# Spreading the softmax denominators of three head groups through DRAM in a one-core decoder kernel

## The reference

```python
att = jnp.einsum('bhqd,bhkd->bhqk', q, k) * scale
att = jnp.where(causal[None, None], att, -jnp.inf)
y = jnp.einsum('bhqk,bhkd->bhqd', jax.nn.softmax(att, axis=-1), v)
attc = jnp.einsum('bhqd,bhkd->bhqk', qc, kc) * scale
y = y + jnp.einsum('bhqk,bhkd->bhqd', jax.nn.softmax(attc, axis=-1), vc)
y = y.transpose(0, 2, 1, 3).reshape(x.shape[0], T, C)
return y @ Wp + bp
```

## Time and profile before

| what | value |
|---|---|
| median of 3 runs | 2014.0 us (2013.98 to 2019.18) |
| profiled execution, its own time | 2022.06 us |
| its span, first to last instruction | 2020.2 us |
| TensorE busy | 1575.8 us (78%) |
| VectorE busy | 1434.7 us (71%) |
| ScalarE busy | 833.2 us (41%) |
| GpSimd busy | 654.7 us (32%) |
| mean granted TensorE clock | 0.889 |

### The profile page before, as it was taken

One profiled execution on the slowest core, in us unless ns is written; L12 is line 12 of the kernel. 1 busy time (PEld: TensorE's weight loads), 2 busy tenths in 40 slices (PEclk: granted clock), 3 DMA queues, 4 the chain that ended last, 5 costly groups with the idle time before them and its releaser, 6 DMA issues. The chain is left out here.

```text
span 2020.2 us, 19779 instructions
## 1 busy us (share of the span) xinstructions
PE 1575.8 (78%) x6792; PEld 757.8 (38%) x6792; DVE 1434.7 (71%) x2096; ACT 833.2 (41%) x1570; POOL 654.7 (32%) x423
## 2 busy tenths in 40 slices
PE   4796799884987699874977799855567898669985
PEld 2353332232544222242544223232232222348874
DVE  6996778657995878468986877389968776333324
ACT  4541246645442166644432365543312566322211
POOL 2664501212763401125653211227635021112221
PEclk9898789996998699987998699988987899769998
DMA  5910722003001820002004520021007220127753
GB/s 167 342 51 0 177 41 41 1 1 116 17 1 49 168 34 8 2 32 98 4 0 123 94 40 2 1 84 43 0 0 159 38 41 1 64 89 252 232 180 127
DMA packets 121189, 147.46 MB, mean 73 GB/s; under 512 B 15429, under 2 KB 103886, under 8 KB 119040
## 3 DMA queue, kind: packets, MB, share of 16 engines
q1 hardware_dynamic: 117344, 137.53, 25.4%
q0 software_dynamic: 3744, 8.66, 1.2%
HBM read 96.79 MB, written 50.79 MB: 73 GB/s over the span
## 5 line engine op out<-in xcount | busy, mean ns | idle before, releaser
L168 PE MATMUL PS<-arena 128*32 128x512 f32 (+11 forms) x4150 | 884.4, 453 | 105.2 <-DVE maxs L1724 24.4
L168 PEld LDWEIGHTS PS<-arena 128*32 128x32 f32 (+3 forms) x4150 | 368.9, 128 | 597.7 <-ACT arena L1705 276.4
L1705 ACT ACTIVATE arena<-PS 128x512 f32<-128x512 f32 (+3 forms) x768 | 375.4, 541 | 379.9 <-PE PS L168 378.7
L1354 POOL TENSOR_TENSOR arena<-arena 128x1024 f32<-128x1024 f32 x128 | 305.0, 2384 | 238.0 <-DVE arena L1380 140.4
L1724 DVE TENSOR_REDUCE maxs<-PS 128x1 f32<-128x1024 f32 x256 | 302.1, 1216 | 80.9 <-PE PS L168 80.8
L1380 DVE TENSOR_TENSOR_SCAN arena<-PS,arena 128x1024 f32<-128x1024 f32 x128 | 292.2, 2283 | 6.1 <-ACT PS L1329 6.1
L168 PE MATMUL PS<-arena,ident 128*128 128x512 f32 (+1 forms) x560 | 260.1, 590 | 5.4 <-DVE arena L1389 5.4
L1329 ACT ACTIVATE PS<-arena,A_neg 128x511 f32<-128x511 f32 x256 | 165.9, 681 | 237.4 <-DVE arena L1380 188.0
L1558 POOL TENSOR_TENSOR arena<-xn 128x512 f32<-128x512 f32 x16 | 20.2, 1266 | 590.9 <-ACT xn L1693 590.9
L1389 DVE TENSOR_TENSOR arena<-arena,PS 128x1024 f32<-128x1024 f32 x128 | 156.3, 1221 | 7.3 <-PE PS L168 3.2
L168 PE MATMUL PS<-bc,bc_sel 96*128 96x512 bf16 x128 | 52.5, 410 | 120.0 <-DVE arena L1389 113.5
(11 more groups left out here) (261 smaller groups left out, 1796.6 us busy)
## 6 DMA issues: line engine op xcount, KB each, us to landing
arena<-in_ew SPq DMA_DIRECT2D x46, 512.0 KB, 4.9
arena<-stack_parts SPq DMA_DIRECT2D x288, 64.0 KB, 3.9
rows_in<-nil SPq DMA_DIRECT2D x16, 1088.0 KB, 12.5
arena<-b_rows SPq DMA_DIRECT2D x16, 1024.0 KB, 7.6
stack_parts<-arena SPq DMA_DIRECT2D x40, 384.0 KB, 3.1
arena<-stack_parts SPq DMA_DIRECT2D x96, 128.0 KB, 4.7
arena<-rows_in SPq DMA_DIRECT2D x23, 272.0 KB, 5.4
arena<-picked_rows SPq DMA_DIRECT2D x16, 256.0 KB, 3.2
```

The source lines that it names most:

```text
L168: return nc.tensor.matmul(o, l, r, start=start, stop=stop)
L1354: nc.gpsimd.tensor_tensor(b_sb[i % 2], u[:, 2 * kh:2 * kh + 2, :], Brow[:, n, :].unsqueeze(1).to_broadcast([P, 2, T]), ALU.mult).then_inc( ...
L1705: nc.scalar.activation(probs[(HG * s + h) % NPR][:, 0:N], bank(4 + n % 2)[:, 0:N], ACT.Exp, scale=HD ** -0.5).then_inc(S["ring_read"], 1)
```

## The change

TensorE and ScalarE no longer spread the denominators of groups 0 to 2. When ScalarE has copied a group's sums, SyncE stores the four denominator rows of `Y1` and `Y2` to a DRAM tensor `dens`, waits for both stores, and loads each of its two halves into `den_sb` with every row repeated 32 times. GpSimd waits for the loads (`dens_in`). The last group keeps the selector matmuls and copies; its copy also waits for the inverse of group 2. The ring's numbering loses the tiles of the removed matmuls, by twos, so the banks still alternate as before. The semaphore `bp_added`, for which nothing waited, is gone.

```diff
+    dens = nc.dram_tensor("dens", (2, HG, T), F32).ap()
...
         def ring(g, k, h):
-            return HG * (STEPS * g + k) + h + 2 * max(g - 1, 0) + (2 if g >= 1 and k >= 2 else 0)
+            return HG * (STEPS * g + k) + h
 
-        def ring_den(g, i):
-            return HG * STEPS * (g + 1) + 2 * g + i + (2 * HG if g + 1 < NG else 0)
+        def ring_den(i):
+            return HG * STEPS * NG + i
...
+                def load_denominators(g):
+                    sp.wait_ge(S["pv_copied"], g + 1)
+                    for i, y in enumerate((Y1, Y2)):
+                        sp.dma_start(dens[i], y[HD:P:32, :]).then_inc(S["dens_out"], 16)
+                    sp.wait_ge(S["dens_out"], 32 * (g + 1))
+                    for i in range(2):
+                        sp.dma_start(den_sb[:, i, :], dens[i].unsqueeze(1).to_broadcast([HG, 32, T]))\
+                            .then_inc(S["dens_in"], 16)
+
                 sp.wait_ge(S["pv_mm"], STEPS)
+                load_denominators(0)
                 load_stacks(sp, 3)
-                load_max_rows(2)
+                load_max_rows(2, (0,))
+                load_max_rows(2, (1,))
+                load_denominators(1)
                 load_max_rows(3)
+                load_denominators(2)
...
                 for g in range(NG):
-                    pool.wait_ge(S["ring_read"], ring_den(g, 1) + 1)
+                    if g + 1 < NG:
+                        pool.wait_ge(S["dens_in"], 32 * (g + 1))
+                    else:
+                        pool.wait_ge(S["ring_read"], ring_den(1) + 1)
...
-                        if k == 1 and g >= 1:
-                            denominators(g - 1)
                         if k >= 1:
                             values(g, k - 1)
...
                 values(NG - 1, STEPS - 1)
-                denominators(NG - 1)
+                last_denominators()
...
-                def copy_denominators(g):
+                def copy_last_denominators():
+                    act.wait_ge(S["norm_ready"], NG - 1)
...
-                    if g >= 1 and k == 1:
-                        copy_denominators(g - 1)
                 copy_sums(NG - 1)
-                copy_denominators(NG - 1)
+                copy_last_denominators()
```

More of the change, by code:

```diff
@@ L298, in decoder @@
             bc3_ready dt_mm abs_done sp_ready cn_mm gen_in pow_mm pow_ev b_src_ready b_stored b_ready a_done
-            h_done g_done y_mm y_read u_ready outproj_mm bp_added qkv_mm hi_f_ready mid_ready parts_ready v_mm
+            h_done g_done y_mm y_read u_ready outproj_mm dens_out dens_in qkv_mm hi_f_ready mid_ready parts_ready v_mm
             v_init v_ready ones_ready max_mm max_done mt_mm mt_read mparts_ready ring_mm ring_read pv_mm
@@ L915, in tensor @@
                     if ends:
-                        pe.wait_ge(S["ring_read"], ring_den(NG - 1, 1) + 1)
+                        pe.wait_ge(S["ring_read"], ring_den(1) + 1)
                     for m in range(2 * DT):
@@ L1474, in gpsimd @@
                 pool.wait_ge(S["xn_ready"], TT)
-                nc.gpsimd.tensor_tensor(x1[:], x1[:], bp[:].unsqueeze(1).to_broadcast([P, TT, DM]), ALU.add)\
-                    .then_inc(S["bp_added"], 1)
+                nc.gpsimd.tensor_tensor(x1[:], x1[:], bp[:].unsqueeze(1).to_broadcast([P, TT, DM]), ALU.add)
                 for i in range(len(TILES)):
@@ L1612, in scores, with last_denominators @@
                         last.then_inc(S["ring_mm"], 1)
-                def denominators(g):
-                    pe.wait_ge(S["pv_copied"], g + 1)
+                def last_denominators():
+                    pe.wait_ge(S["pv_copied"], NG)
                     for i, y in enumerate((Y1, Y2)):
-                        pe.wait_ge(S["ring_read"], ring_den(g, i) - 1)
-                        mm(bank(4 + ring_den(g, i) % 2), den_sel[:], y, True, True).then_inc(S["ring_mm"], 1)
+                        pe.wait_ge(S["ring_read"], ring_den(i) - 1)
+                        mm(bank(4 + ring_den(i) % 2), den_sel[:], y, True, True).then_inc(S["ring_mm"], 1)
                 def values(g, k):
@@ L1687, in copy_sums @@
                     nc.scalar.activation(Y2, bank(7), ACT.Copy).then_inc(S["pv_copied"], 1)
-                def copy_denominators(g):
+                def copy_last_denominators():
+                    act.wait_ge(S["norm_ready"], NG - 1)
                     for i in range(2):
-                        n = ring_den(g, i)
+                        n = ring_den(i)
                         act.wait_ge(S["ring_mm"], n + 1)
```

## The result

| | before | with the change |
|---|---|---|
| median | 2015.26 us (4 runs, 2013.98 to 2019.18) | 2036.72 us (4 runs, 2034.54 to 2040.1) |
| ratio | | 1.0101, 95% interval 1.0082 to 1.012 |
| profiled execution, its span | 2022.06, 2020.2 us | 2034.54, 2032.8 us |
| TensorE busy | 1575.8 us | 1551.1 us |

A forecast was written before the change was run, and what follows sets the result against it. TensorE was taken to set the pace in the attention. Against a median of 2014.0 us, minus 15.3, plus 13.6, minus 8.4, plus 9.8 made -0.3, so 2013.7 us, range 1989 to 2027.

The forecast's parts named there:

- Minus 15.3, plus 13.6: Groups 1 and 2: 15.3 us won by removing the selector matmuls, 13.6 given back to late denominators.
- 8 x 1.7 = 13.6: VectorE's reciprocal in groups 1 and 2: denominators 1.7 us late in each of eight places, 13.6 us lost.
- The rest costs nothing: the 24 stack loads ... start some 3.5 us later: Stack loads behind the denominator loads: their later start costs nothing, since their group begins more than 30 us after them.
- four engines, and the way to them: Denominator loads: a source with outer count 4 uses 4 DMA engines, so both land in 7.1 us.
- Rival 1: Denominator loads run on 16 engines, nothing is given back and no clock falls: 1990.3 us, chance 0.18.
- what the removal gives in groups 1 and 2: Heads of groups 1 and 2: removing the selector matmuls wins 1.91 us on TensorE in each of eight places.
- I expect the fall to stay and to cover values and scores in their place: Head of group 3: slow clock remains after the matmuls go, gain 2.1 us in each of four places, 8.4 in all.
- the bound of 3.5 each: Head of group 3: upper bound of the gain in each of four places, if the clock fall disappears.
- the falls behind the new pauses: Groups 1 and 2, after TensorE's wait: clock falls cost 1.6 us each, six of eight places, 9.8 us.
- Rival 3: Groups 1 and 2: denominators 3.2 us late, the pause exceeds what was removed, slower at 2028.7 us, chance 0.22.

The follow-up runs named there:

- e11: The kernel of e1 with the denominator loads cut into four of 128 KB, each with 2 source rows outermost: 2059.34 us, ratio 1.021.
- e2: The changed kernel with each group's denominators loaded by four transfers, one per head, instead of two: 1983.43 us, ratio 0.9862.
- e1: The changed kernel with SyncE waiting for both denominator loads to land before issuing group 3's stack loads: 2011.1 us, ratio 0.9991.
- e3: The changed kernel without the stores and loads of the denominators, so not the full computation: 1984.51 us, ratio 0.9861.
- e10: The kernel of e2 with the selector matmuls and copies returned for group 2 alone: 2001.16 us, ratio 0.9932.
- e4: The changed kernel with VectorE's reciprocal behind the next group's first twelve maxima instead of eight: 1998.15 us, ratio 0.9921.
- e6: The changed kernel with the edits of e1 and e4 together, loads still on four engines: 1988.38 us, ratio 0.9863.
- e8: The changed kernel with the context keys' loads issued last among group 3's stack loads: 2036.15 us, ratio 1.0105.

## Why the prediction was wrong

**The step that failed: "Minus 15.3, plus 13.6".** The term "8 x 1.7 = 13.6" took one lateness for groups 1 and 2. It was 2.0 us in group 2 (1.8 to 2.0 in the four batches) and 8.2 in group 1 (7.9 to 8.6): 4 x 2.0 + 4 x 8.2 = 41 us instead of 13.6. The price of a microsecond of lateness was right (in e11, 7.5 us late, a group takes 49.9 - 40.1 = 9.8 us more, of which 7.5 are the wait and the rest is taken for the slow clock behind it). The error stood in "The rest costs nothing: the 24 stack loads ... start some 3.5 us later": I asked what the new transfers do to the stack loads and not what the stack loads, issued right behind, do to the new ones, and priced a transfer by b_rows, which nothing disturbs. The trace of before had the warning. Its busy time by stretch in group 1, while only the stack loads move:
```profile
311.50:321.50 10.00, 9.40 (x49) 2.33 (x48) 6.80 (x5) 6.68 (x13) 4.98 (x4) 1.00 1.02 150
```
DMA share 1.02 at 150 GB/s: these 24 loads keep all 16 engines busy for some ten microseconds, at a rate well below the 1024 KB in 2.5 us of the earlier trace rows. A load issued just ahead of them was bound to run among them, and that had no term in the sum.

**Right: four engines, and the way to them.** From the 4 short packets of the earlier trace rows I took 4 against 16, and worked out 7.1 us to the landing and a lateness of 1.7; measured, with no stack load near, were 7.3 to 7.7 to GpSimd's start, a lateness of 2.0, and 25.4% of 16 engines. The Trainium skill's rule (DMA: Bandwidth & Descriptors, "Why a DMA increments its semaphore by 16 and not by 1"), that the slowest dimensions of both sides set the number, agrees with the times of e2, e1 and e11. For 4 engines the busy share shows it; for e11 it does too (12.9% of 16 in 362.5 to 372.5, 2.1 engines). For e2 the time alone speaks. Rival 1, 1990.3 with 16 engines, is the kernel e2: 1983.4, and the difference is mostly group 3's.

**Right: what the removal gives in groups 1 and 2.** 41.93 - 40.10 = 1.83 us a group in e3, against 1.91.

**Mis-sized: group 3.** "I expect the fall to stay and to cover values and scores in their place", 2.1 us each. In the change the fall went with the matmuls: 39.1 - 35.1 = 4.0 us (3.8 without the chance part above), about 16 us in all instead of 8.4, even beyond the bound of 3.5 each. e10 brings fall and loss back. Where a fall did come without them (e4, e6), it cost 1.1 to 1.3 us, near the 3.5 - 2.1 = 1.4 that the forecast had for one over values and scores; what it had wrong is that the fall would come each time. The pause before is nearly the same in both kernels; compare the two stretches of the change from group 3's pause on with the earlier trace rows, third and fourth row:
```profile
395.60:399.00 3.40, 2.18 (x14) 0.64 (x13) 2.45 (x4) 3.40 (x7) 0.00 (x0) 1.00 0.00 0
399.00:402.40 3.40, 2.67 (x14) 0.56 (x13) 0.00 (x0) 2.62 (x6) 0.00 (x0) 1.00 0.03 8
```
Nor did the pause alone bring the fall: in the eight places with the matmuls the clock fell between 0.4 us before and 0.9 us after the first of them began. Nor does TensorE's busy time in the pause decide it: it was 2.21 of 3.40 us in e2, without a fall, and 2.21 of 3.40 before the fall in e6. With the selector matmuls TensorE also stands idle some 0.3 us more just before them (1.92 busy in e10), and that was not tried by itself. Why it falls in the one and seldom in the other wasn't settled.

**Right: the falls behind the new pauses.** The stretches of the change around the pause of group 2 (first two) and of group 1:
```profile
368.30:371.70 3.40, 0.86 (x6) 0.11 (x2) 3.40 (x2) 1.09 (x2) 3.24 (x4) 1.00 0.00 0
371.70:375.10 3.40, 2.98 (x14) 0.62 (x14) 3.40 (x4) 1.08 (x2) 0.94 (x1) 0.74 0.02 5
...
327.40:330.80 3.40, 2.84 (x10) 0.91 (x14) 2.91 (x4) 1.08 (x2) 1.16 (x1) 0.50 0.11 30
```
TensorE was busy 0.86 of 3.40 us, where I had 0.9, and in the stretch in which it resumed the mean clock was 0.74 and 0.50. The clock fell in all eight places, where I had six. In group 2 the change takes 43.7 - 40.1 = 3.6 us more than without lateness, 2.0 of them the wait, which leaves 1.6 us for the slow clock, the size of the forecast's. In group 1 it is 50.4 - 40.1 - 8.2 = 2.1. Where e4 had no wait (0.02 us, third batch), there was no fall and group 1 took 40.3 us.

**The sum with the measured terms:** -8 x 1.83 + 41 - 16 + 4 x 1.6 + 4 x 2.1 = +25 us, against 21.5 by the medians and 24.8 by the groups. Rival 3 had the right sign and path (late denominators, a wait longer than what was removed) and the wrong cause: it made all eight places late by a slow store and slow rows, where four were late by their neighbours.

## What to carry to other kernels

Price a new transfer by the traffic it will meet, not by a like one that ran alone: look at what is issued right behind it and whether that alone fills the engines. Lay the slowest dimension of both sides out so that all DMA engines take part; here the transfer was then over before its neighbours mattered (e2). And where a result that arrives late is needed by one instruction in the middle of an in-order program, try moving that instruction: here it cost 0.1 us a group and by itself gave back 36 of the 48 us (e4), and together with holding back the neighbours as much as the fast transfer (e6 against e2).

## What was not expected of the hardware

A transfer is not safe from those issued after it. The two loads were issued at 308.39 and by 309.57, the first stack load at 309.60, and from the first issue to GpSimd's start it was then 13.8 us instead of 7.3 to 7.7; with the small stack loads first behind them it was 12.3. A row of 2 KB took 180 to 210 ns instead of 84 (e8). Whether the rows waited for their neighbours on the same four engines, or at the memory they read or write, was not tried apart; the records don't name the engine.

The pair of f32 selector matmuls cost 3.9 us in group 3 though it takes 1.9 at full clock, because the granted clock fell to half, for 3.4 us, within a microsecond of its beginning, in each of the four batches before and again in each of the four in e10. In the same place without them it fell in 3 of 32.
